# Rotary projection of a fused two-layer kernel: the rotated features are split in two float16 and folded three steps later

## The reference

```python
q_hk = (hidden_q @ Wq.T).reshape(Bv, Sv, H, K)           # 16 heads, K = 128
q_big = jnp.einsum('bshk,hkq->bshq', q_hk, w_kc_q)       # 192 features
q_big = q_big * cos_q + _rotate_half(q_big) * sin_q      # rotary, 192 features
q_r = jnp.einsum('bshq,hqr->bhsr', q_big, W_qr)
k_r = jnp.einsum('bld,hdr->bhlr', kv_r, W_kr)
scores = jnp.einsum('bhsr,bhlr->bhsl', q_r, k_r)
```

## Time and profile before

| what | value |
| --- | --- |
| median of 3 runs | 879.67 us (879.61, 879.67, 888.3) |
| the profiled execution's own time | 878.37 us |
| its span in the trace | 876.6 us |
| mean granted TensorE clock | 0.937 of full |
| PE busy | 732.1 us (84%), 5165 instructions |
| DVE busy | 632.5 us (72%), 1381 instructions |
| ACT busy | 382.6 us (44%), 1209 instructions |
| POOL busy | 357.3 us (41%), 292 instructions |

### The profile page before, as it was taken

The page is one execution under the profiler, slowest core; times in us unless marked ns, Lnnn a source line. Parts: engine busy times, 40 slices in busy tenths (PEclk is TensorE's granted clock), DMA queues, the critical chain, the costliest instruction groups (busy, mean ns, idle before and its releaser), DMA issues. The chain is left out here.

```text
span 876.6 us, 16323 instructions
## 1 busy us (share of the span) xinstructions
PE 732.1 (84%) x5165; PEld 502.8 (57%) x5168; DVE 632.5 (72%) x1381; ACT 382.6 (44%) x1209; POOL 357.3 (41%) x292
## 2 busy tenths in 40 slices
PE   5997999687745548999996899869999999999776
PEld 4664666466612335443442666536878888888544
DVE  4446677656377854665675766659999999999777
ACT  2456656151325312212313655226454555554484
POOL 4301444227024412434353544258656565565210
PEclk9998999988958777999999999969999999999989
DMA  9452000000020002022000300011010101002101
GB/s 256 121 187 84 1 0 0 1 1 1 0 85 1 1 19 84 21 64 85 0 1 25 121 0 0 0 30 26 25 31 18 36 18 36 18 18 83 64 1 49
DMA packets 26637, 35.31 MB, mean 40 GB/s; under 512 B 10208, under 2 KB 18400, under 8 KB 25696
## 3 DMA queue, kind: packets, MB, share of 16 engines
q1 hardware_dynamic: 26592, 34.74, 12.9%
HBM read 33.68 MB, written 1.05 MB: 40 GB/s over the span
## 5 line engine op out<-in xcount | busy, mean ns | idle before, releaser
L1616 POOL TENSOR_TENSOR ra_direct<-ra_direct,ra_crossed 128x512 f32<-128x512 f32 x64 | 81.5, 1273 | 87.0 <-DVE ra_crossed L1760 87.0
L636 ACT ACTIVATE c_probs<-bank,c_neg_max 128x128 f32<-128x128 f32 x256 | 90.1, 379 | 60.2 <-DVE c_neg_max L688 60.2
L1760 DVE SCALAR_TENSOR_TENSOR ra_crossed<-bank,ra_bias,ra_sin 64x512 f32<-64x512 f32 x128 | 96.0, 750 | 1.9
L655 POOL TENSOR_TENSOR c_probs<-c_probs,c_inverse 128x512 f32<-128x512 f32 x64 | 65.3, 1040 | 71.2 <-DVE c_inverse L670 71.2
L1263 POOL TENSOR_TENSOR r_turned<-r_times_a,r_times_b 128x1024 f32<-128x1024 f32 x24 | 56.4, 2349 | 92.1 <-DVE r_times_b L1441 92.1
L601 PE MATMUL bank<-l_out_mat,c_ctx_t 128*128 128x256 f32 x256 | 61.8, 385 | 8.5 <-DVE c_ctx_t L699 8.5
L688 DVE TENSOR_REDUCE c_neg_max<-bank 128x4 f32<-128x512 f32 x64 | 41.5, 685 | 27.8 <-PE bank L65 27.8
L601 PEld LDWEIGHTS bank<-l_out_mat,c_ctx_t 128*128 128x128 f32 x256 | 46.2, 190 | 18.5 <-issue 8.4
L1719 ACT ACTIVATE ra_probs_t<-bank 128x512 f32<-128x512 f32 x32 | 19.1, 598 | 84.9 <-PE bank L1665 84.9
L636 ACT ACTIVATION_READ_ACCUMULATOR c_probs<-bank,c_neg_max 128x1 f32 x256 | 55.7, 218 | 0.0
L1724 ACT ACTIVATE ra_probs<-ra_masked,ra_neg_max 128x128 f32<-128x128 f32 x128 | 49.8, 390 | 11.1 <-DVE ra_neg_max L1779 10.7
(11 more groups left out here) (237 smaller groups left out, 2053.7 us busy)
## 6 DMA issues: line engine op xcount, KB each, us to landing
ra_raw<-l_attn_w_dram SPq DMA_DIRECT2D x16, 384.0 KB, 3.1
wq<-l_wq_dram SPq DMA_DIRECT2D x16, 256.0 KB, 3.0
wo<-l_wo_dram SPq DMA_DIRECT2D x16, 256.0 KB, 3.4
wkcq<-l_wkcq_dram SPq DMA_DIRECT2D x16, 192.0 KB, 3.1
ra_wo<-l_attn_wo_dram SPq DMA_DIRECT2D x1, 2048.0 KB, 9.7
wqr<-l_wqr_dram SPq DMA_DIRECT2D x16, 96.0 KB, 3.3
x_res<-x_dram SPq DMA_DIRECT2D x2, 512.0 KB, 4.2
wkv<-l_wkv_dram SPq DMA_DIRECT2D x16, 64.0 KB, 3.0
```

The lines of the kernel that those rows point to most:

```text
L636: e = nc.scalar.activation(probs[u][:, n, :], score_bank[q][:, n - q * HP, :], ACT.Exp, bias=neg_max[u][:, n:n + 1], accum_out=total[u][:, ...
L655: nc.gpsimd.tensor_tensor(out=probs[u][:, at, :], in0=probs[u][:, at, :], in1=inverse[u][:, at].unsqueeze(2).broadcast_to([P, HP, L]), op= ...
L1616: nc.gpsimd.tensor_tensor(out=direct[e][k][:], in0=direct[e][k][:], in1=crossed[k][:], op=ALU.add).then_inc(roped, 1)
L1760: ins = nc.vector.scalar_tensor_tensor(dst[out_lo:out_lo + rows].rearrange("p t (b s) -> p (t b) s", b=2), src[lo:lo + rows], bias[v][lo:l ...
```

## The change

The rotated features are split: POOL still adds `times_a` and `times_b` into `turned` (two buffers now), ACT copies that to float16 (`turned_hi`), POOL subtracts (`turned_lo`). The weights `a` are split too: ACT copies to float16 (`inner_hi`, `outer_hi`), DVE subtracts (`inner_lo`, `outer_lo`; a new `keep_a` on DVE, six instructions, before the loop and at place 3). The fold is three float16 products in place of a float32 one. It comes three steps late instead of two (`LAG`), and `high` and `low` of the latent banks move from place modulo 3 = 1 to place modulo 3 = 2. In ACT's stream the copy of step k - 1, `turn_high(k - 1)`, stands first in step k, ahead of `high`, `keep_g`, `keep_a` and `keep_o`. In POOL's stream the order is add(0), add(1), low(0), add(2), low(1) and so on, and behind the last add low(22), low(23).

```diff
+    LAG = 3
...
-        fold_outer = [sb(f"fold_outer{v}", [P, 2, 2, P]) for v in range(2)]
-        fold_inner = [sb(f"fold_inner{v}", [P, 2, DC]) for v in range(2)]
+        outer_hi = [sb(f"outer_hi{v}", [P, 2, 2, P], F16) for v in range(2)]
...
-        turned = [sb(f"turned{r}", [P, 2, TH * P]) for r in range(3)]
+        turned = [sb(f"turned{r}", [P, 2, TH * P]) for r in range(2)]
+        turned_hi = [sb(f"turned_hi{r}", [P, 2, TH * P], F16) for r in range(LAG + 1)]
+        turned_lo = [sb(f"turned_lo{r}", [P, 2, TH * P], F16) for r in range(LAG + 1)]
...
             for v in range(2):
-                nc.gpsimd.memset(fold_outer[v][:], 0.0).then_inc(cleared, 1)
+                for outer in (outer_hi[v], outer_lo[v]):
+                    nc.gpsimd.memset(outer[:], 0.0).then_inc(cleared, 1)
             ln.gpsimd(pool)
+
+            def low(k):
+                pool.wait_ge(turned_high, k + 1)
+                r = k % (LAG + 1)
+                nc.gpsimd.tensor_tensor(out=turned_lo[r][:], in0=turned[k % 2][:], in1=turned_hi[r][:],
+                                        op=ALU.subtract).then_inc(turned_low, 1)
+
             for k in range(STEPS):
                 pool.wait_ge(multiplied, 2 * k + 2)
-                wait(pool, folded, k - 2)
-                nc.gpsimd.tensor_tensor(out=turned[k % 3][:], in0=times_a[k % 2][:], in1=times_b[k % 2][:],
+                wait(pool, turned_low, k - 1)
+                nc.gpsimd.tensor_tensor(out=turned[k % 2][:], in0=times_a[k % 2][:], in1=times_b[k % 2][:],
                                         op=ALU.add).then_inc(rotated, 1)
+                if k:
+                    low(k - 1)
+            low(STEPS - 1)
...
-                pe.wait_ge(rotated, k + 1)
+                pe.wait_ge(turned_low, k + 1)
+                r = k % (LAG + 1)
                 if c == 1:
                     for w in range(2):
-                        for e in range(2):
...
+                        for x, y in ((inner_hi, turned_hi), (inner_lo, turned_hi), (inner_hi, turned_lo)):
+                            for e in range(2):
+                                rows, cols = slice(e * HD, (e + 1) * HD), slice((1 - e) * HD, (2 - e) * HD)
+                                mm = nc.tensor.matmul(latent_bank[e][cols, :], x[v][rows, w, :], y[r][rows, w, :],
...
                     for w in range(2):
-                        mm = nc.tensor.matmul(latent_bank[e][:], fold_outer[v][:, w, e, :], turned[k % 3][:, w, :],
-                                              start=(w == 0), stop=(w == 1))
-                    mm.then_inc(folded, 1)
+                        factors += split_factors(outer_hi[v][:, w, e, :], outer_lo[v][:, w, e, :],
+                                                 turned_hi[r][:, w, :], turned_lo[r][:, w, :])
+                    mm = accumulate(nc, latent_bank[e][:], factors)
+                mm.then_inc(folded, 1)
...
-                if k >= 2:
-                    fold(k - 2)
+                if k >= LAG:
+                    fold(k - LAG)
...
+            def turn_high(k):
+                act.wait_ge(rotated, k + 1)
+                wait(act, folded, k - LAG)
+                nc.scalar.activation(turned_hi[k % (LAG + 1)][:], turned[k % 2][:],
+                                     ACT.Copy).then_inc(turned_high, 1)
...
-                if place % NCH == 1 and k >= NCH:
+                if k:
+                    turn_high(k - 1)
+                if place % NCH == 2 and k >= NCH:
                     for side in range(2):
                         high(k // NCH - 1, side)
...
+            def keep_a(quad):
+                v = quad % 2
+                dve.wait_ge(a_hi, quad + 1)
+                nc.vector.tensor_tensor(inner_lo[v][:], a_bank[:, :, 1, :], inner_hi[v][:], ALU.subtract)
+                for c, p0, rows, side in KEPT:
...
+                ins.then_inc(a_kept, 1)
...
             for e in range(2):
                 keep_g(0, e)
+            keep_a(0)
             ln.lows(dve)
...
                 rotate(k, 0)
-                if place % NCH == 1 and k >= NCH:
+                if place % NCH == 2 and k >= NCH:
                     low(k // NCH - 1, 0)
                 rotate(k, 1)
-                if place % NCH == 1 and k >= NCH:
+                if place % NCH == 2 and k >= NCH:
                     low(k // NCH - 1, 1)
                 if quad + 1 < QUADS and place in (0, 2):
                     keep_g(quad + 1, place // 2)
+                if quad + 1 < QUADS and place == 3:
+                    keep_a(quad + 1)
```

More of the change, by code:

```diff
@@ L1220, in cross_project_rotary @@
         big_lo = [sb(f"big_lo{v}", [P, CC, 2, NCH * P], F16) for v in range(2)]
-        fold_outer = [sb(f"fold_outer{v}", [P, 2, 2, P]) for v in range(2)]
-        fold_inner = [sb(f"fold_inner{v}", [P, 2, DC]) for v in range(2)]
+        outer_hi = [sb(f"outer_hi{v}", [P, 2, 2, P], F16) for v in range(2)]
+        outer_lo = [sb(f"outer_lo{v}", [P, 2, 2, P], F16) for v in range(2)]
+        inner_hi = [sb(f"inner_hi{v}", [P, 2, DC], F16) for v in range(2)]
+        inner_lo = [sb(f"inner_lo{v}", [P, 2, DC], F16) for v in range(2)]
         times_a = [sb(f"times_a{r}", [P, 2, TH * P]) for r in range(2)]
         times_b = [sb(f"times_b{r}", [P, 2, TH * P]) for r in range(2)]
-        turned = [sb(f"turned{r}", [P, 2, TH * P]) for r in range(3)]
+        turned = [sb(f"turned{r}", [P, 2, TH * P]) for r in range(2)]
+        turned_hi = [sb(f"turned_hi{r}", [P, 2, TH * P], F16) for r in range(LAG + 1)]
+        turned_lo = [sb(f"turned_lo{r}", [P, 2, TH * P], F16) for r in range(LAG + 1)]
         table_a, table_b = sb("table_a", [P, NCH, 2, S]), sb("table_b", [P, NCH, 2, S])
@@ L1232, in cross_project_rotary @@
         g_done, g_hi, g_lo = g.sem("r1_g_done"), g.sem("r1_g_hi"), g.sem("r1_g_lo")
-        a_done, a_kept = g.sem("r1_a_done"), g.sem("r1_a_kept")
+        a_done, a_hi, a_kept = g.sem("r1_a_done"), g.sem("r1_a_hi"), g.sem("r1_a_kept")
+        turned_high, turned_low = g.sem("r1_turned_high"), g.sem("r1_turned_low")
         o_done, o_kept = g.sem("r1_o_done"), g.sem("r1_o_kept")
@@ L1328, in fold @@
                     pe.wait_ge(a_kept, unit // 2 + 1)
-                pe.wait_ge(rotated, k + 1)
+                pe.wait_ge(turned_low, k + 1)
+                r = k % (LAG + 1)
                 if c == 1:
                     for w in range(2):
-                        for e in range(2):
[L1333 to L1336, removed]
-                    mm.then_inc(folded, 1)
+                        for x, y in ((inner_hi, turned_hi), (inner_lo, turned_hi), (inner_hi, turned_lo)):
+                            for e in range(2):
+                                rows, cols = slice(e * HD, (e + 1) * HD), slice((1 - e) * HD, (2 - e) * HD)
+                                mm = nc.tensor.matmul(latent_bank[e][cols, :], x[v][rows, w, :], y[r][rows, w, :],
+                                                      start=False, stop=(w == 1 and y is turned_lo),
+                                                      skip_group_check=True)
                 else:
@@ L1340, in fold @@
                     wait(pe, q_lo, 4 * unit - 2 + 2 * e)
+                    factors = []
                     for w in range(2):
-                        mm = nc.tensor.matmul(latent_bank[e][:], fold_outer[v][:, w, e, :], turned[k % 3][:, w, :],
-                                              start=(w == 0), stop=(w == 1))
-                    mm.then_inc(folded, 1)
+                        factors += split_factors(outer_hi[v][:, w, e, :], outer_lo[v][:, w, e, :],
+                                                 turned_hi[r][:, w, :], turned_lo[r][:, w, :])
+                    mm = accumulate(nc, latent_bank[e][:], factors)
+                mm.then_inc(folded, 1)
             for e in range(2):
@@ L1363, in _ @@
                         multiply_o(quad + 1)
-            for k in (STEPS - 2, STEPS - 1):
+            for k in range(STEPS - LAG, STEPS):
                 fold(k)
@@ L1382, in keep_a @@
                 if quad < 2:
-                    act.wait_ge(cleared, 2)
-                nc.scalar.activation(fold_inner[v][:], a_bank[:, :, 1, :], ACT.Copy)
+                    act.wait_ge(cleared, 4)
+                nc.scalar.activation(inner_hi[v][:], a_bank[:, :, 1, :], ACT.Copy)
                 for c, p0, rows, side in KEPT:
-                    e = nc.scalar.activation(fold_outer[v][p0:p0 + rows, :, c // 2, side * DC:(side + 1) * DC],
+                    e = nc.scalar.activation(outer_hi[v][p0:p0 + rows, :, c // 2, side * DC:(side + 1) * DC],
                                              a_bank[p0:p0 + rows, :, c, :], ACT.Copy)
-                e.then_inc(a_kept, 1)
+                e.then_inc(a_hi, 1)
+            def turn_high(k):
[3 more added lines that the diff above has]
+                                     ACT.Copy).then_inc(turned_high, 1)
             def keep_o(quad):
@@ L1418, in _ @@
```

(7 more changed lines are left out.)

## The result

The changed kernel takes 894.01 us (median of 20 runs), the kernel before, in the same comparisons, 881.6. The kernel is slower by a little over 1%, outside what I had called likeliest; the median lies 0.01 us above the stated range of 877 to 894, and the medians differ by 12.4 us where I had forecast 6.2.

The account below looks back on a forecast made before the run. The prediction took PE to bound the stage before, and a loop through POOL, ACT and DVE after. Terms 0.4 + 0.6 + 3.75 + 1.45 = +6.2 us on 879.67 gave 885.9 us, range 877 to 894.

Parts of the forecast that it names:

- The bound of the kernel before: In the stage, before the change: it goes at PE's pace, PE busy 29.8 of 32 and 31.7 of 34 us.
- PE's saving: PE's folds: six float16 passes for eight, 0.43 us in each of 24 folds, 10.3 us, expected off the path.
- The ring: Loop from POOL's add through ACT's turn_high and high, DVE's low and rotate, to the next add: 5.0 us a unit.
- POOL's part: POOL's adds and subtractions in each three-step unit: 11.15 us, so no unit shorter than 16.2.
- The units with a and o: Units at places 3 to 5, with DVE's six new subtractions at 1.4 us: 17.0 us each.
- rival 4: DVE binds: six subtractions at 0.55 us each, or rotates put off more; +7.6 us, 893.5; chance 13%.
- The unit given 16.7 for its late weights: Unit beginning with g, whose weights SP asks for only after o: middle add late, 16.7 us.
- All six: The six units from add(5) to add(23): 99.45 us against 99.0, +0.4.
- Before the loop: DVE's six subtractions stand in PE's wait before o: +1.45 us.
- Behind the loop: From the start of add(23) to the last high: 8.1 us against 4.38, +3.75.
- The third rival: Clock falls in PE's holes in the last quad and behind: 903.6 us, one unit alone 893.3; chance 9%.
- The first rival: PE stays the bound, the loop through ACT being looser and units following PE: -4.3 us, 875.4; chance 9%.

Follow-up runs that it names:

- e1: Changed kernel with ACT's four high copies moved ahead of turn_high(k - 1) in steps with k modulo 3 = 2; 884.21 us, ratio to before 1.0053.
- second execution: The changed kernel itself, nothing altered, profiled once more (the run also called e10); 889.03 us.
- e4: Changed kernel with extra float16 matmuls in PE's waits, 14 before fold(21) and 15 before fold(22); median 893.32 us.
- e11: e9 with SP asking for the weights of g, a and o as soon as each is done; 869.58 us, ratio 0.9863.
- e7: Kernel before, with folds three steps late and two transposes ahead of o, float32 folds, no split; 880.57 us, ratio 0.9982.
- e12: e7 with SP asking for the weights of g, a and o as soon as each is done; 873.91 us, ratio 0.9905.
- e9: Changed kernel with high ahead of turn_high, two transposes ahead of o, split only in quads 0 to 2, float32 folds in the last; 879.74 us, ratio 0.9978.
- e6_combined: Changed kernel with high ahead of turn_high, two transposes ahead of o, and the last two subtractions on DVE; 881.97 us, ratio 1.0003.
- first execution of the changed kernel: The changed kernel itself, nothing altered, in its first profiled execution; 901.88 us.
- e10: The changed kernel itself, nothing altered, one more execution; 889.03 us.
- e3: Changed kernel without POOL's subtraction and without the third product, with turned_lo; 876.6 us, ratio 0.9954.

## Why the prediction was wrong

Point by point, by its own steps.

- **The bound of the kernel before, and PE's saving.** Right. An outer fold takes 6 x 0.215 in the trace, and the 10.3 us did not come out, as forecast.
- **The ring.** Right in mechanism, shown by e1. "That is 5.0 us": it took 5.1 in the second execution, from 470.20 (end of an add) to 475.30:

```profile
467.85 2.35 POOL L1278 TENSOR_TENSOR r_turned<-r_times_a,r_times_b 128x1024 f32<-128x1024 f32 x1
...
470.24 1.06 ACT L1414 ACTIVATE r_turned_hi<-r_turned 128x1024 f16<-128x1024 f32 x1 [3.52 <-POOL r_turned L1278]
471.32 2.45 ACT L1426 ACTIVATE l_q_stack<-bank 64x512 f16<-64x512 f32 x4
472.56 1.41 DVE L1492 TENSOR_TENSOR l_q_stack<-bank,l_q_stack 64x512 f16<-64x512 f32 x2 [4.05 <-ACT l_q_stack L1426]
474.00 1.23 DVE L1481 TENSOR_TENSOR r_times_b<-bank,r_table_b 128x1024 f32<-128x1024 f32 x1
475.26 1.41 DVE L1492 TENSOR_TENSOR l_q_stack<-bank,l_q_stack 64x512 f16<-64x512 f32 x2
475.30 2.34 POOL L1278 TENSOR_TENSOR r_turned<-r_times_a,r_times_b 128x1024 f32<-128x1024 f32 x1 [3.02 <-DVE r_times_b L1481]
```

- **POOL's part, "2.31 + 2.09 + 2.31 + 2.09 + 2.35 = 11.15".** Mis-sized. The 2.09 came from a pair; here an add follows its subtraction after 2.27. Two of these make 0.36 a unit. With the ring's 0.1 a plain unit is 16.5 to 16.6, not 16.2. The units with a and o came at 17.4 for 17.0. Their extra term had DVE's six subtractions at 1.4; they take 1.7 (rival 4 had 3.3). The unit given 16.7 for its late weights took 17.4; its third add, and not only its middle one, came late, 1.03 us, for a rotate that stood behind PE's late g. All six: +2.7 in place of +0.4.
- **Before the loop, "+1.45".** The six subtractions lengthened the wait by 1.7; the other 0.4 are transposes at half the clock, which I had not counted. Behind them stood a term that I had at zero: the first bigs at half the clock, +1.3 (six matmuls start 0.43 us apart in place of 0.215). No run held the clock up here, so this price is read from the rows alone.
- **Behind the loop, "+3.75".** The chain is right to the tenth: 8.09 measured with the clock held up (e4), 8.1 forecast. The clock adds 0.9 in one execution and 1.9 in the other. I had this in the range ("the last two folds at the lower clock 3") and left it out of the sum.

**The step that failed** is therefore not the mechanism but the size of the sum: +6.2 forecast, +11.7 measured for the stage in the second execution. Two terms were at fault, POOL's part of a unit, taken too short, and the TensorE clock at both ends of the loop, put at nothing. About 2.3 of the missing 5.5 are the loop's terms, 0.3 the six subtractions before it, and some 2.6 the clock at the loop's two ends (0.4 + 1.3 + 0.9); 0.3 are in steps 0 to 5. The third rival had the clock fall in the last quad's holes, and weighed against it "stretches with 1.7 to 2 us of holes"; the earlier trace rows give 2.2 and 2.3. There it held at 1.00 for most of the time (438 to 472 us in the second execution); in the first it fell behind a wait of 2.04 us in the last quad, and the units stayed at 16.5 and 16.6. What it cost lay elsewhere: it rose late before the loop, fell behind the loop, and in some executions behind the late weights. The chances for the outcome, 0.62 for within 1%, were set by a sum with such terms at zero; all of them could only have one sign.

The first rival (PE stays the bound) is refuted for this order of the work, and nearly true for e11's.

## What to carry to other kernels

An instruction moved ahead on an in-order engine passes its wait to everything behind it, so follow the queue until it comes back to its own start: a ring's length divided by what it produces is a bound that no engine's busy share shows. Here two swapped lines gave back over half of what it cost. A saving on the busiest engine pays only when the next wait behind it goes too, here a transfer asked for by one wait for all; asking sooner lowered the ratio by 0.8% (e7 to e12) and 1.2% (e9 to e11). When a change opens a hole of some us in PE's stream, price the work behind it at half the clock as a term of the sum, not as an accident: in the tail this was 0.9 us in one execution and 1.9 in the other.

## What the runs showed of the hardware that I had not expected

DVE's subtraction with both inputs in SBUF was held up while POOL worked; I had this only as a condition in the expectation of e6_combined. There the first of two began at 468.05 us, while POOL's add lasted until 466.65 + 2.34 = 468.99:

```profile
468.05 3.29 DVE L1528 TENSOR_TENSOR r_turned_lo<-r_turned,r_turned_hi 128x1024 f16<-128x1024 f32 x2
```

The group of this line in the same run (least, median and most ns of one, then when the two began):

```profile
L1528 DVE TENSOR_TENSOR r_turned_lo<-r_turned,r_turned_hi x2: 1226/1627/2028, 468.0 to 470.1; 128x1024 f16<-128x1024 f32 x2
```

The first took 2.03 us, the second, alone, 1.23. By the Trainium skill, SBUF — State Buffer, "SBUF: two separate sides", a DVE operation with two inputs in SBUF and a POOL operation that reads SBUF take turns by a lock for a whole instruction. The trace agrees: the extra 0.80 is about the 0.94 that POOL's add still had to go. It is one instruction in one run. DVE's rotates, with one input in the accumulation banks, took 1.21 to 1.23 us throughout, beside POOL or not. Moving POOL's subtractions to DVE wholesale would therefore hardly make the two engines independent; that wasn't tried.

What stays open is when the clock falls. Behind the late weights it fell in the first execution of the changed kernel, e9, e6 and e1, after waits of 2.03, 2.69, 2.74 and 3.09 us; it did not in e10 after 1.70, nor in e7 after 2.01. In e3 it fell behind two waits of 2.40 us for low, and not behind a third of the same length nor behind one of 2.72. So the length of the last wait alone does not decide it.
